# W1's loads interleaved with the first group's copies in a compressed-interaction kernel; pair sums and products reordered

## The reference, cut to what matters

```python
# input: (512, 64, 16) f32 = (batch, field, d); W0 (128, 64*64), W1 and W2 (128, 64*128), b (128,)
x_vec = input
for W, b in ((W0, b0), (W1, b1), (W2, b2)):
    z = jnp.einsum('bhd,bfd->bhfd', x_vec, input)          # products of every row of x_vec with every field
    z = z.reshape(B, h * f, d)
    x_vec = jnp.einsum('oc,bcd->bod', W, z) + b[None, :, None]
    outs.append(x_vec.sum(axis=2))
return jnp.concatenate(outs, axis=1)                       # (512, 384)
```

## Time and profile before

| what | value |
|---|---|
| runs before | 1140.29 us median of 3 (1138.67 to 1140.75) |
| profiled execution | 1139.53 us, span 1137.7 us, mean granted clock 0.991 |
| PE | 1096.1 us busy (96%) |
| DVE, ACT, POOL | 868.1 (76%), 453.2 (40%), 840.5 (74%) |
| DMA | 86.89 MB, mean 76 GB/s |

### The profile page before, as it was taken

The page is one execution under the profiler, slowest core; times in us unless marked ns, Lnnn a source line. Parts: engine busy times, 40 slices in busy tenths (PEclk is TensorE's granted clock), DMA queues, the critical chain, the costliest instruction groups (busy, mean ns, idle before and its releaser), DMA issues.

```text
span 1137.7 us, 16831 instructions
## 1 busy us (share of the span) xinstructions
PE 1096.1 (96%) x4589; PEld 775.6 (68%) x4589; DVE 868.1 (76%) x3002; ACT 453.2 (40%) x1532; POOL 840.5 (74%) x762
## 2 busy tenths in 40 slices
PE   2899999999999999999999999999999999999996
PEld 2477666676668666666668666766667766766776
DVE  3356978888794888979794797978887588888991
ACT  2244434444341443434352343434443253443550
POOL 3766796979784797878876688787978479697551
PEclk9989999999999999999999999999999999999998
DMA  7861423314051141514142051423313133240000
GB/s 248 249 165 40 93 72 68 91 27 123 24 122 44 34 115 23 124 35 112 54 93 56 17 115 51 95 70 72 94 29 102 35 81 85 41 111 15 1 1 28
DMA packets 112350, 86.89 MB, mean 76 GB/s; under 512 B 75136, under 2 KB 75776, under 8 KB 112128
## 3 DMA queue, kind: packets, MB, share of 16 engines
q1 hardware_dynamic: 109376, 75.27, 27.6%
q10 hardware_dynamic: 2880, 10.55, 2.6%
HBM read 14.75 MB, written 0.79 MB: 14 GB/s over the span
## 4 chain that ended last, share of the span: by engine, by line
PE 83%; DVE 11%; DMA 3%; issue 2%; POOL 1%; ACT 0%; SPq 0%; POOLq 0%
PE y L644 54%; PE l L656 19%; DVE acc L584 8%; PE xt L679 5%; PE l2p L691 3%; DMA xg<-in_r_input_dram 2%; DVE bd L551 2%; DMA z<-xg 1%; DVE x1l L559 1%; PE l2p L668 1%; PE xt L661 1%; PE y L733 0%; PE l L652 0%; POOL z L337 0%; DVE acc L582 0%
## 5 line engine op out<-in xcount | busy, mean ns | idle before, releaser
L584 DVE SCALAR_TENSOR_TENSOR acc<-y,x0t,acc 128x128 f32<-128x128 f32 x2560 | 699.2, 340 | 201.6 <-PE y L644 198.9
L490 ACT ACTIVATE prod<-y,x0t 128x128 f32<-128x128 f32 x1280 | 367.6, 371 | 607.0 <-PE y L644 573.8
L644 PE MATMUL y<-w1h,x1h 128*128 128x512 f32 x1024 | 509.3, 497 | 6.2 <-DVE acc L584 4.3
L644 PE MATMUL y<-w1h,x1l 128*128 128x512 f32 x1024 | 404.3, 395 | 0.0
L644 PE MATMUL y<-w1l,x1h 128*128 128x512 f32 x1024 | 403.7, 394 | 0.0
L348 POOL TENSOR_TENSOR pacc<-pacc,prod 128x512 f32<-128x512 f32 x192 | 247.1, 1287 | 183.8 <-ACT prod L490 183.8
L337 POOL TENSOR_TENSOR z<-z,xg 128x512 f32<-128x512 f32 (+1 forms) x272 | 353.0, 1303 | 25.7 <-DMA z<-xg 25.5
L644 PEld LDWEIGHTS y<-w1h,x1h 128*128 128x128 f32 x1024 | 193.4, 189 | 136.5 <-issue 60.3
L656 PE MATMUL l<-z,w0t 128*128 128x512 f32 x512 | 262.6, 594 | 2.7 <-POOL z L337 2.7
L644 PEld LDWEIGHTS y<-w1l,x1h 128*128 128x128 f32 x1024 | 193.6, 189 | 81.1 <-issue 54.3
L644 PEld LDWEIGHTS y<-w1h,x1l 128*128 128x128 f32 x1024 | 192.6, 188 | 44.1
(11 more groups left out here) (50 smaller groups left out, 278.4 us busy)
## 6 DMA issues: line engine op xcount, KB each, us to landing
z<-xg SPq DMA_DIRECT2D x512, 128.0 KB, 2.4
xg<-in_r_input_dram SPq DMA_DIRECT2D x32, 128.0 KB, 3.8
w2t<-in_L_rec_W_dram ACTq DMA_DIRECT2D x8, 512.0 KB, 12.4
gram<-in_L_rec_W_dram ACTq DMA_DIRECT2D x8, 512.0 KB, 8.6
z<-xg SPq DMA_DIRECT2D x16, 192.0 KB
gram<-in_L_rec_W_dram ACTq DMA_DIRECT2D x1, 2048.0 KB, 7.9
out_dram<-z SPq DMA_DIRECT2D x4, 192.0 KB, 2.1
b1r<-in_L_rec_b_dram ACTq DMA_DIRECT2D x1, 64.0 KB, 10.0
```

What stands on the lines that cost most here:

```text
L490: last = nc.scalar.activation(prod[:, h % HSLOTS, k, :], y[c % YB][:, k * O:(k + 1) * O], ACT.Copy, scale=x0t[:, j, f:f + 1])
L584: ins = nc.vector.scalar_tensor_tensor(out=to, in0=of, scalar=x0t[:, j, f:f + 1], in1=b1r[:] if m == 0 else to, op0=ALU.mult, op1=ALU.add)
L644: ins = nc.tensor.matmul(to, stationary, moving, start=(first and k == 0), stop=(last and k == 2))
```

## The change

W1's eight loads are no longer issued together at the start. ScalarE waits for group 0's `xg`, issues two parts, and issues one more behind each landed copy t = 0, 2, 4, 6, 8 and 10. The lists of steps are new: "w0" steps stand right ahead of the `layer0` steps that need them, "w1" steps begin only behind `layer0` step 10 (W1_AFTER), two behind each further `layer0` step, and the last `layer0` step (t = 16) stands behind "w1" 12 on TensorE and behind "w1" 10 on the others. VectorE makes the pair sums of shifts 0 to 26 and GpSimd those of 27 to 32, so GpSimd reaches its products after 13 instructions in place of 33. W2 is turned behind the chunks from e = 12 on in place of e = 10. SP's program is the same.

```diff
+W_PARTS = 8
+W1_FIRST = 2
-W2_AT = 10
-W1_LEAD = 3
+W2_AT = 12
+W1_AFTER = 10
+LEFT_AFTER, LEFT_LATER = 10, 12
-POOL_PAIRS = 17
+POOL_PAIRS = 27
...
-        def steps_before(lead):
-
-            steps = [("w0", r, r % YB) for r in range(W0_STEPS)]
-            for i in range(CHUNKS + lead):
-                if i < CHUNKS:
-                    steps.append(("w1", i, i % YB))
-                steps += [("l0", t, None) for t in range(ZT) if t * CHUNKS // ZT == i - lead]
+        def steps_before(left_after):
+
+            steps, turned = [], 0
+            for t in range(ZT - 1):
+                if t % 4 == 0:
+                    steps.append(("w0", t // 4, turned % YB))
+                    turned += 1
+                steps.append(("l0", t, None))
+                if t == W1_AFTER - 1:
+                    steps.append(("w0", W0_STEPS - 1, turned % YB))
+                    turned += 1
+                if t >= W1_AFTER:
+                    for i in range(2 * (t - W1_AFTER), 2 * (t - W1_AFTER) + 2):
+                        steps.append(("w1", i, turned % YB))
+                        turned += 1
+                        if i == left_after:
+                            steps.append(("l0", ZT - 1, None))
+            for i in range(2 * (ZT - 1 - W1_AFTER), CHUNKS):
+                steps.append(("w1", i, turned % YB))
+                turned += 1
+                if i == left_after:
+                    steps.append(("l0", ZT - 1, None))
             return steps
...
-            load(w1raw, w1, w1_loaded)
+            act.wait_ge(xg_loaded, 32)
+            for k in range(W1_FIRST):
+                load(w1raw, w1, k, w1_loaded)
...
                     if r == ZT - 1:
                         left_parts(0)
+                    elif r % 2 == 0 and W1_FIRST + r // 2 < W_PARTS:
+                        act.wait_ge(b_loaded[zslot(r)], 32 * (r // ZSLOTS + 1))
+                        load(w1raw, w1, W1_FIRST + r // 2, w1_loaded)
```

More of the change, by code:

```diff
@@ L189, in cin_kernel @@
         W0_STEPS = -(-ZT // 4)
-        def steps_before(lead):
-            steps = [("w0", r, r % YB) for r in range(W0_STEPS)]
-            for i in range(CHUNKS + lead):
-                if i < CHUNKS:
-                    steps.append(("w1", i, i % YB))
-                steps += [("l0", t, None) for t in range(ZT) if t * CHUNKS // ZT == i - lead]
+        def steps_before(left_after):
[19 more added lines that the diff above has]
+                    steps.append(("l0", ZT - 1, None))
             return steps
-        PREP, PE_PREP = steps_before(0), steps_before(W1_LEAD)
+        PREP, PE_PREP = steps_before(LEFT_AFTER), steps_before(LEFT_LATER)
         def turned_in(steps):
@@ L390, in _, with load @@
             act.sem_inc(prod_made, HN)
[L392 to L396, removed]
+            def load(to, of, k, loaded):
+                part = F * O // W_PARTS
+                act.dma_start(to[:, k * part:(k + 1) * part], of[:, k * part:(k + 1) * part]).then_inc(loaded, 16)
             act.dma_start(w0raw, w0).then_inc(w0_loaded, 16)
@@ L498, in _ @@
                         left_parts(0)
+                    elif r % 2 == 0 and W1_FIRST + r // 2 < W_PARTS:
+                        act.wait_ge(b_loaded[zslot(r)], 32 * (r // ZSLOTS + 1))
+                        load(w1raw, w1, W1_FIRST + r // 2, w1_loaded)
                     continue
                 if (what, r) == ("w1", W2_LOADED_AT):
-                    load(w2raw, w2, w2_loaded)
+                    for part in range(W_PARTS):
+                        load(w2raw, w2, part, w2_loaded)
                 act.wait_ge(prep_made, turned_in(PREP[:k]) + 1)
@@ L715, in _ @@
                     if r % 4 == 0:
-                        pe.wait_ge(y_used[(r // 4) % YB], uses(PE_PREP[:r // 4 + 1], (r // 4) % YB))
+                        at = [step[:2] for step in PE_PREP].index(("w0", r // 4))
+                        kept = PE_PREP[at][2]
+                        pe.wait_ge(y_used[kept], uses(PE_PREP[:at + 1], kept))
                     layer0(0, r)
@@ L720, in _ @@
                 if (what, r) == ("w1", 0):
-                    pe.wait_ge(w1_loaded, 16 * 8)
+                    pe.wait_ge(w1_loaded, 16 * W_PARTS)
                 if uses(PE_PREP[:k], bank):
@@ L752, in body @@
                         if e == W2_AT:
-                            pe.wait_ge(w2_loaded, 16 * 8)
+                            pe.wait_ge(w2_loaded, 16 * W_PARTS)
                         turn_w2(e - W2_AT)
```

## The result

The changed kernel takes 1151.01 us (median of 4 runs, 1149.43 to 1151.71), the kernel before 1140.24 beside it (4 runs). The ratio is 1.009, 95% interval 1.0077 to 1.0104: slower, and above the range that I gave, 1138.0 to 1148.0. The profiled execution took 1149.43 us, the fastest of the four, with a span of 1147.7 us (1137.7 before).

A forecast was written before the change was run, and what follows sets the result against it. TensorE bounds the kernel (83% of the last-ending chain); the change acts ahead of group 0's first chunk and shortly behind. +2.35, +1.15 and +0.1 give +3.6 on 1137.7, 1141.3; 1143.9 us against the median, range 1138.0 to 1148.0.

The forecast's parts named there:

- xg: Group 0's load, no longer sharing with W1, lands at about 13 (12.3 to 13.7) in place of 25.1.
- Pair sums, W2_AT: VectorE's 20 further sum instructions cost nothing (3 us without cover); later W2 turns meet the same waits, 0.1 us added.
- The copies and W1: Ahead of W1's turning: last part issued at 35 behind copy 10, W1 in at 38.5, bounds 34.5 and 43.
- The factor of 1.24: W2 and copies together took 6.7 us where separate prices give 5.4; on all of W1's stretch, 39.4 for 34.6.
- The turning: W1's turns on TensorE, 14.3 us with 2.3 for low clock, then W2's issues: group 0 at 61.9, 2.35 us later.
- W2 and group 1's xg: xg meets W2 packet for packet, lands at 68.2 for 63.15; TensorE's first layer-0 step of group 1 3.5 us late.
- The sum: Whole span: +2.35 for group 0's start, +1.15 for group 1's xg, +0.1, so +3.6 us.
- Rival 1: W1's parts and the copies hinder each other more, W1 in at 41 to 43: 1147 to 1148.5 us; chance 0.10.
- Rival 2: Interleaved parts fill idle DMA time, W1 in at 34.5: 1139.9 us, or 1137.6 with high clock; chance 0.22.
- Rival 4: The biases' small packets hold group 0's xg, copies start at 16 or later: 1147 us; chance 0.05.
- Rival 3: Group 0's xg lands at about 10: 3 us less, 1140.9 us, no difference; chance 0.08.

The follow-up runs named there:

- e4: The kernel before with POOL_PAIRS = 27 alone, so VectorE makes the pair sums of shifts 0 to 26: 1139.80 us, ratio 1.0.
- e8: The kernel before with W2_AT = 12 alone, so the turns of W2 move two chunks back: 1139.19 us, ratio 0.9995.
- e1: The changed kernel with all eight parts of W1 issued at once behind group 0's xg: 1148.99 us, ratio 1.0084.
- e2: The changed kernel with W2's eight issues moved behind the last x1h work, right ahead of group 0: 1156.25 us, ratio 1.0147.
- e3: The kernel before with one wait added, so group 0's xg loads ahead of W1's eight loads: 1142.50 us, ratio 1.0026.
- e6: The kernel before with W2's loads issued behind all casts of W1 and zleft, ahead of the x0t copy: 1143.93 us, ratio 1.0035.
- e10: e9 with W2's eight loads issued together ahead of the cast of "w1" 13: 1144.84 us, ratio 1.0041.
- e12: e9 with W2's parts issued one by one ahead of the casts of "w1" 2 to 9: 1136.36 us, ratio 0.9972.
- e11: e9 with W2's parts issued one by one ahead of the casts of "w1" 4 to 11: 1137.39 us, ratio 0.9979.
- e5: The changed kernel with W2 issued ahead of the cast of "w1" 4 in place of 13: 1143.32 us, ratio 1.0028.
- e9: Changed kernel: W1 at once behind xg, "w0" steps first, "w1" from behind layer-0 step 4, W2's parts singly ahead of casts "w1" 7 to 14: 1138.80 us.
- e7: e6 with two xg buffers, so group n+1's xg is issued right behind group n's copies: 1143.25 us, ratio 1.0028.

## Why the prediction was wrong

The direction and most of the places were right; the size was 3.6 us on the span and is 10.0. Against the medians the forecast of 1143.9 missed by 7.1. In order of the prediction's steps:

**xg.** Forecast 12.3 to 13.7, measured 11.35, and the first copy is issued then. I had it share the engines until 10; in 9:10 q1 moved 1606 packets beside one of q10, also more than the 1156 per us that I took. The sooner landing bought nothing by itself.

**Pair sums, W2_AT.** Forecast nothing or 0.1; e4 and e8 show nothing in the kernel before.

**The copies and W1: this step failed.** I let 11 copies and seven parts, 20.1 us of engine time, pass ahead of the last part, and so had W1 in at 38.5. But nothing in the change holds SP back: it had issued the copies up to t = 15 by 32.93 and the last by 33.63, all ahead of W1's last part at 35.19. What the engines had to move before the last part landed was nearly everything: 4.32 MB of copies and 3.92 MB of W1 in 14 to 42, at a share of 1.05. The issue at 35.19 was right to 0.2 us by luck, as two rows show:

```profile
33.65 1.27 POOL L355 TENSOR_TENSOR z<-z,xg 128x512 f32<-128x512 f32 x1 [0.45 <-DMA z<-xg]
35.19 0.26 ACT L532 CAST w0left<-y 96x128 fp32r<-96x128 f32 x1 [2.18 <-PE y L751]
```

Copy 10, the one I had the part wait for, is in by 33.65, where its product starts. The part was issued together with the cast of `w0left`, for which ScalarE had waited for TensorE's last "w0" step behind product 9. That is the wait of which I had written that it doesn't bind. The 3.5 us that I gave from the issue to the landing were 7.8. W1 came in at 43.03, 4.5 us late, at the upper bound of the step. The factor of 1.24 in that step was wrong in the other direction: over the whole stretch it is 1.07 (28 us for 26.3).

**The turning.** Right: the clock was 0.50 in its first 3 us (43:46), and from W1 in to W2's first issue it took 58.12 − 43.07 = 15.05 us, against 53.5 − 38.5 = 15.0. Part of that closeness is luck: "w1" 12 was turned 0.7 us later than I had it (58.08 − 43.07 = 15.0 for 14.3), and W2's first issue went out beside its cast and not 0.7 us behind it. For the low clock I took 2.3 us; against e1 it is 1.9. The issues were on the path, as said, but 4.0 us long (58.12 to 62.14) and not 5.09. That took 1.1 us off the start of group 0: 65.47, where 61.9 + 4.5 would be 66.4.

**W2 and group 1's xg.** The mechanism was right and the chain of sums too: W2 issued at 53.5, `xg` at 68.2, was 14.7 us; measured 58.12 and 73.6, 15.5. Six kernels in which `xg` met a W2 issued all together give one number. From W2's first issue to `xg`'s landing it took 15.5 us in the changed kernel, 15.2 in e1 (56.49 to 71.69), 15.2 in e2 (64.03 to 79.19), 15.5 in e3 (51.81 to 67.34), 15.6 in e6 (50.74 to 66.30) and 15.8 in e10 (52.60 to 68.36). So `xg` lands when W2 is through and its own rest, some 3 us, behind it (in the changed kernel q10's last packets are in 70:71 and `xg` is in at 73.6). The Trainium skill's page "DMA: Bandwidth & Descriptors", section "Queues, rings and completion order", has an engine take turns between its queues packet by packet, and typically drain some 9 to 17 descriptors of a queue, one packet in its sense, before it switches. The turns are there: 102 against 102 in 69:70, and 198 against 200 in e2. But what goes in one turn is a single run of 64 bytes for one packet of weights, not 9 to 17 of them, so on that figure the measurement decides against the page.

**The sum.** TensorE's first layer-0 step of group 1 came 8.8 us late (78.06 against 69.25) where I had 3.5: 4.5 of the difference is W1, 0.8 the term just named. Behind that wait of 2.87 us came what I had left out. The clock fell to 0.50 again, the step took 2.04 us in place of 0.86 and the next six matmuls 2.01 where the same six took 1.40 in e12 and e11: 1.8 us. 8.8 + 1.8 is the 10.6 of the fence on groups 2 and 3. I had 0.1 for all behind that step: a term that I put at nothing without a reason, though I had priced the same clock behind the wait for W1. At the end of the span the shift is 10.0, since the last 128 transposes took 16.01 us in this execution and 16.63 in that of before:

```profile
1126.18 16.01 PE xt L702 x128
```

That stretch the change doesn't touch. It takes 15.95 to 17.46 us over all traces of this case, 15.95 in e4 and 15.99 in e8, so it varies between executions of kernels that leave it alone; why is open.

**The rivals.** Rival 1 had W1 in at 41 to 43, where it was, but for another reason: the two hinder each other little beyond their sum (28 us for 26.3), there was only more of the sum. Its 1147 to 1148.5 lacked the second low clock. Rival 2's case, turning from near 35 on, never came in the changed kernel. e10 reaches it with another list and W2 in its old place, turns from 34.62 on, and takes 1144.84, where I had priced it at 1137.6 to 1139.9: group 1's `xg` beside W2 takes the gain. That e11 and e12, at 1137.4 and 1136.4, come near that price is no support for it, since they moved W2 as well. Rival 4 falls: the biases don't hold `xg`. Rival 3's early `xg` came half true (11.35, between 10 and 13) without its gain, since the copies' issue is not what is late; e3 shows the same.

What could be won back lay elsewhere, as e5 and e9 to e12 show: in putting W1's turns beside the copies' landing, as in the kernel before (4.1 us, e1 against e10), and W2 ahead of group 1's `xg` (7.7 us in e5, 6.0 to 8.5 in e9, e11 and e12 against e10). In the changed kernel's own list all parts at once were 2.0 us better than parts and copies in turns (e1); in e12's list the turns weren't tried.

## What to carry to other kernels

To price a transfer, count all that the other queues will have issued ahead of its last packet, not only what the program's order puts ahead of it: a queue whose waits are all met runs ahead. In these runs a load of many small packets cost its own time plus all of the large load that it met (15.2 to 15.8 us behind W2's first issue, where alone it takes 3.5), so move the large load to where the small one isn't, and ask at once which transfer it meets there (e2, e6 and e7 each moved it into the next one). When a late load can't be made sooner, reorder what waits for it, so that the work behind the one transfer covers the other. And price what TensorE does behind each new wait at the clock that such waits leave it: 1.8 to 1.9 us for each of the two here.

## What the chip showed that was not expected

W1's first packets are slow. In the changed kernel its first two parts are issued from 11.36 on, and in 12:13 q10 moved 18 packets at a share of 105.4%: they occupied all the engines and moved 0.07 MB in that microsecond, where 0.39 MB went in 69:70. Of the copies, issued from 11.35 on, no packet moved before 14.

```profile
q10 hardware_dynamic: 18, 0.07, 105.4%
```

W2's eight issues took ScalarE 5.09 us in the kernel before, 4.0 in the changed kernel and in e10, 4.34 in e2 and e6, and 0.33 to 0.36 each (2.7 in all) where they stood apart, in e9, e11 and e12; why is open. And behind the wait of 2.87 us TensorE came back at half its clock (the stretch 78:81 above), so that this wait cost 4.7 us in all.
